# Layer 3's feed-forward: the gate product on VectorE out of its PSUM bank, and its steps in a new order

## What is computed

```
g = silu(einsum('th,ehi->tei', xf, w_gate))
u = einsum('th,ehi->tei', xf, w_up)
experts_y = einsum('tei,eih->teh', g * u, w_down)
y = sum over the 2 picked experts of experts_y * weight
shared = silu(x @ sw_gate) * (x @ sw_up) @ sw_down
x = x + tanh(g_ffn[3]) * (y + shared)
```

## Time and profile before

| | |
|---|---|
| runs | 932.77, 924.78, 932.22 us; median 932.22 |
| the profiled execution | 930.15 us, of which the span of its instructions is 928.4 us |
| PE busy | 841.6 us (91% of the span) |
| DVE busy | 763.0 us (82%) |
| ACT busy | 555.4 us (60%) |
| POOL busy | 309.8 us (33%) |

### The profile page before, as it was taken

How to read it: one execution, slowest core, us unless ns; L and a number is a source line. 1 busy time by engine, 2 the same in 40 slices (tenths; PEclk the granted TensorE clock), 3 DMA queues, 4 the chain that set the end, 5 groups by cost and what they waited for, 6 DMA issues and landing times.

```text
span 928.4 us, 16914 instructions
## 1 busy us (share of the span) xinstructions
PE 841.6 (91%) x5288; PEld 651.5 (70%) x5288; DVE 763.0 (82%) x1907; ACT 555.4 (60%) x1077; POOL 309.8 (33%) x507
## 2 busy tenths in 40 slices
PE   5998887899999999999999999999979989978796
PEld 3776756666666665688878788778767779867574
DVE  6899899869999998699889899788887755465886
ACT  3777565547777775675666565577755534423474
POOL 2644226313444433232222122433421253321143
PEclk9999999759999997999999999999998999997998
DMA  5000000000000000010000000020001000000001
GB/s 155 9 2 1 4 26 1 25 1 26 26 25 26 22 23 1 9 42 0 1 1 1 1 1 1 0 76 2 1 2 43 1 1 1 1 1 1 1 12 34
DMA packets 26005, 14.12 MB, mean 15 GB/s; under 512 B 11047, under 2 KB 25406, under 8 KB 25918
## 3 DMA queue, kind: packets, MB, share of 16 engines
q1 hardware_dynamic: 25758, 13.04, 5.1%
q10 hardware_dynamic: 160, 0.00, 0.0%
HBM read 11.99 MB, written 1.05 MB: 14 GB/s over the span
## 4 chain that ended last, share of the span: by engine, by line
PE 47%; DVE 8%; issue 3%; ACT 3%; POOL 0%; DVEq 0%; ACTq 0%; POOLq 0%
PE bank L1844 4%; PE bank L1846 3%; PE bank L1845 3%; PE bank L798 2%; PE bank L1319 2%; PE bank L1900 2%; PE bank L1901 2%; PE bank L1899 2%; PE bank L1274 2%; PE bank L1284 2%; PE bank L1297 1%; PE bank L1255 1%; PE bank L731 1%; PE bank L709 1%; PE bank L758 1%
## 5 line engine op out<-in xcount | busy, mean ns | idle before, releaser
L893 ACT ACTIVATE L_pt<-bank 128x512 f32<-128x512 f32 x224 | 127.2, 598 | 46.4 <-PE bank L767 32.5
L515 POOL TENSOR_TENSOR L_kc<-L_kc_all,const 128x256 fp32r<-128x256 f32 x96 | 59.7, 625 | 141.7 <-PE bank L767 81.9
L1026 DVE TENSOR_REDUCE L_ms<-bank 128x2 f32<-128x512 f32 x128 | 84.0, 685 | 11.8 <-PE bank L716 11.4
L1801 POOL TENSOR_TENSOR L1f_xg_lo<-L1f_xg_raw,L1f_xg_hi 128x512 fp32r<-128x512 f32 x32 | 42.0, 1313 | 145.3 <-ACT L1f_xg_hi L1949 141.3
L880 ACT ACTIVATE L_part<-bank,L_bias_ca,const 128x256 fp32r<-128x256 f32 x128 | 68.9, 563 | 33.8 <-PE bank L687 32.4
L2065 DVE TENSOR_TENSOR L1f_h_lo<-L1f_h,L1f_h_hi 128x512 fp32r<-128x512 f32 x88 | 75.2, 859 | 6.2 <-ACT L1f_h_hi L1954 5.9
L1943 ACT ACTIVATE L1f_a<-bank 128x512 f32<-128x512 f32 x88 | 52.4, 599 | 43.3 <-PE bank L1846 42.9
L1024 DVE TENSOR_REDUCE L_mc<-bank 128x8 f32<-128x512 f32 (+1 forms) x96 | 65.1, 678 | 8.7 <-PE bank L709 4.4
L1954 ACT CAST L1f_h_hi<-L1f_h 128x512 fp32r<-128x512 f32 x88 | 54.3, 618 | 18.8 <-DVE L1f_h L2060 18.8
L716 PE MATMUL bank<-L_k,L_q 32*128 32x256 f32 x256 | 55.9, 342 | 5.1 <-DVE L_ms L1026 4.9
L887 ACT ACTIVATE L_hm<-bank,const 128x256 fp32r<-128x256 f32 x96 | 45.6, 475 | 21.5 <-PE bank L731 20.6
(11 more groups left out here) (427 smaller groups left out, 2601.1 us busy)
## 6 DMA issues: line engine op xcount, KB each, us to landing
L_raw<-in_L_ffn_w_dram SPq DMA_DIRECT2D x8, 176.0 KB, 2.3
L_raw<-in_L_ffn_v_dram SPq DMA_DIRECT2D x8, 176.0 KB, 2.5
L_raw<-in_L_ffn_w_dram SPq DMA_DIRECT2D x6, 192.0 KB, 2.9
x<-in_x_dram SPq DMA_DIRECT2D x4, 256.0 KB, 4.3
mask<-in_mask_Bx1xSxS_ff_dram SPq DMA_DIRECT2D x2, 512.0 KB, 5.6
out_dram<-x SPq DMA_DIRECT2D x4, 256.0 KB, 2.3
const<-in_const_dram SPq DMA_DIRECT2D x1, 964.0 KB, 6.0
ctx_rows<-in_ctx_dram SPq DMA_DIRECT2D x1, 256.0 KB, 3.1
```

Of the source, the lines that this page charges most:

```text
L515: pool.tensor_tensor(kc[:, g], kc_all[:, g, bass.ds(b, 1)].bitcast(F32).to_broadcast([P, GH, S2]), pr.c("head4").unsqueeze(2).to_broadcast ...
L893: act.activation(pt[:, g // 2, (g % 2) * NS + (HEADS_1[i] if own_keys else i)], b_st[(g * NS + i) % 2][:], ACT.Exp, scale=scale).then_inc( ...
L1026: dve.tensor_reduce(ms[:, :, i - 1], bank.rearrange("p (t s) -> p t s", s=S), AX_X, ALU.max).then_inc(sem["sc_taken"], 1)
```

## The change

ACT's `gate` step and POOL's `mul` step go, and with them the tile `gb` and the semaphore `gate_copied`. DVE's `mul` step, which did nothing in layer 3, now multiplies `h` by the gates straight out of their bank. PE's `gate` matmul waits for the product of the gated chunk two before it, where it waited for the copy out of that bank.

```diff
 gpsimd:
-        def mul(n):
-            ...
-            pool.wait_ge(sem["gate_copied"], past["gate_copied"] + g + 1)
-            pool.tensor_tensor(h[:, n % RH], h[:, n % RH], gb[:, g % 2], ALU.mult).then_inc(sem["h_done"], 1)
 tensor, gate(n):
-                need(pe, sem["gate_copied"], g - 1, past["gate_copied"])
+                need(pe, sem["h_done"], GATED[g - 2] + 1 if g >= 2 else 0, past["h_done"])
             pe.matmul(b_gate[g % 2][:], sel[:, c * P:(c + 1) * P], gts[:, i], start=True, stop=True).then_inc(sem["gate_done"], 1)
 scalar:
-        def gate(n):
-            ...
-                act.copy(gb[:, g % 2], b_gate[g % 2][:]).then_inc(sem["gate_copied"], 1)
 vector:
         def mul(n):
             if layer == 3:
+                dve.wait_ge(sem["half_done"], past["half_done"] + n + 1)
+                if n not in GATED:
+                    dve.wait_ge(sem["h_done"], past["h_done"] + n)
+                    dve.sem_inc(sem["h_done"], 1)
+                    return
+                g = gated_before(n)
+                dve.wait_ge(sem["gate_done"], past["gate_done"] + g + 1)
+                dve.tensor_tensor(h[:, n % RH], h[:, n % RH], b_gate[g % 2][:], ALU.mult).then_inc(sem["h_done"], 1)
                 return
 PLACES, "tensor":
-        (('att3', 'divide', 7, 1), *of("ffn3", ('turn', 2), ('logits', 2)), *of("att3", ('y', 7))),
+        (('att3', 'pv', 7, 1), *of("ffn3", ('logits', 2)), *of("att3", ('y', 7))),
 ...
```

More of the change, by code:

```diff
@@ L2116, in ffn_wide @@
         3: (("lo", 12, 34, "xt_hi xt_lo xt_raw sel yt"), ("arena", 86, 108, "h xn mv ve rstd router extra total total2 total3"), ("hi", 25, 34, "a"),
[L2117 removed]
+            ("arena", 32, 48, "gx pe p1 cand top8 want left picked gs gtop gwant gleft"), ("arena", 0, 32, "gts h_hi h_lo hg"))}[layer])
     mv = sb("mv", [P, NT, 2])
@@ L2393, in y_copy @@
             act.copy(yt[:], b_y[:]).then_inc(sem["yt_ready"], 1)
-        return {"turn": turn, "route": route, "gates": gates, "up": up, "gate": gate, "split": split, "y_copy": y_copy}
+        return {"turn": turn, "route": route, "gates": gates, "up": up, "split": split, "y_copy": y_copy}
     def vector(dve):
@@ L2841 @@
[L2841 to L2854, removed]
+        (('att3', 'divide', 3, 1), *of("att3", ('pv', 3, 1))),
+        (('att3', 'weights', 4, 1), *of("att3", ('proj', 5, 1))),
@@ new lines @@
+        (('att3', 'divide', 4, 0), *of("att3", ('divide', 4, 1), ('turn', 6), ('pv', 4, 0))),
+        (('att3', 'weights', 5, 0), *of("att3", ('context_values', 6))),
+        (('att3', 'divide', 5, 0), *of("att3", ('divide', 5, 1), ('pv', 5, 0), ('turn', 7))),
+        (('att3', 'pv', 5, 1), *of("att3", ('context_values', 7), ('proj', 7, 0))),
+        (('att3', 'y', 5), *of("att3", ('divide', 6, 0))),
+        (('att3', 'maxima', 7), *of("att3", ('divide', 6, 1), ('pv', 6, 0))),
+        (('ffn3', 'logits', 0), *of("att3", ('sums', 7), ('pv', 7, 0))),
@@ new lines @@
+        (('att3', 'divide', 7, 0), *of("att3", ('divide', 7, 1)), *of("ffn3", ('turn', 2), ('logits', 1))),
+        (('att3', 'pv', 7, 1), *of("ffn3", ('logits', 2)), *of("att3", ('y', 7))),
+        (('ffn3', 'up', 1), *of("ffn3", ('up', 2), ('up', 3))),
+        (('ffn3', 'turn', 3), *of("ffn3", ('up', 4))),
+        (('ffn3', 'gates', 0), *of("ffn3", ('gate', 0))),
+        (('ffn3', 'up', 5), *of("ffn3", ('gate', 1))),
+        (('ffn3', 'gate', 3), *of("ffn3", ('up', 7), ('up', 8))),
+        (('ffn3', 'down', 0), *of("ffn3", ('up', 9), ('gates', 2), ('gate', 5))),
@@ new lines @@
+        (('ffn3', 'down', 2), *of("ffn3", ('up', 10))),
+        (('ffn3', 'gate', 6), *of("ffn3", ('gate', 7), ('up', 11))),
+        (('ffn3', 'down', 4), *of("ffn3", ('up', 12))),
+        (('ffn3', 'down', 5), *of("ffn3", ('up', 13), ('gate', 10), ('gate', 11), ('down', 6), ('down', 7), ('up', 14), ('up', 15))),
+        (('ffn3', 'y_turn', 0), *of("ffn3", ('gate', 12), ('gate', 13))),
+        (('ffn3', 'up', 17), *of("ffn3", ('gates', 3))),
+        (('ffn3', 'down', 8), *of("ffn3", ('down', 9))),
@@ L2950 @@
         (('att3', 'maxima', 3), *of("att3", ('turn', 4), ('p_moments', 3))),
+        (('att3', 'scores', 4, 0), *of("att3", ('parts', 3))),
         (('att3', 'maxima', 4), *of("att3", ('turn', 5))),
[L2952 to L2955, removed]
+        (('att3', 'divide', 3, 0), *of("att3", ('divide', 3, 1)), *of("ffn3", ('moments', 0))),
@@ new lines @@
+        (('att3', 'y', 3), *of("att3", ('turn', 6))),
+        (('att3', 'maxima', 5), *of("att3", ('scale', 7)), *of("ffn3", ('prepare',))),
+        (('att3', 'y', 4), *of("ffn3", ('scale', 0)), *of("att3", ('turn', 7))),
+        (('att3', 'scores', 7, 0), *of("att3", ('parts', 6))),
+        (('att3', 'scores', 7, 1), *of("ffn3", ('moments', 1))),
+        (('att3', 'divide', 6, 1), *of("ffn3", ('moments', 2))),
+        (('att3', 'parts', 7), *of("ffn3", ('turn', 0), ('turn', 1))),
+        (('att3', 'divide', 7, 0), *of("att3", ('divide', 7, 1)), *of("ffn3", ('turn', 2))),
@@ L2972 @@
+        (('ffn3', 'gates', 3), *of("ffn3", ('up', 17), ('mul', 15), ('mul', 16))),
+        (('ffn3', 'split', 15), *of("ffn3", ('up', 19))),
+        (('ffn3', 'mul', 17), *of("ffn3", ('mul', 18), ('y_turn', 1), ('mul', 19))),
+        (('ffn3', 'split', 19), *of("ffn3", ('y_turn', 2))),
     ),
@@ L3071 @@
-        (('ffn3', 'up', 17), *of("ffn3", ('gate', 12))),
-        (('ffn3', 'split', 11), *of("ffn3", ('gate', 13))),
-        (('ffn3', 'y_copy', 1), *of("ffn3", ('gate', 15), ('gate', 16))),
-        (('ffn3', 'gate', 14), *of("ffn3", ('up', 18))),
-        (('ffn3', 'split', 14), *of("ffn3", ('gate', 17), ('gate', 18), ('up', 19))),
+        (('att3', 'turn', 6), *of("att3", ('maxima', 5), ('weights', 5, 0))),
+        (('att3', 'divide', 4, 1), *of("att3", ('context_values', 6))),
+        (('att3', 'maxima', 6), *of("att3", ('turn', 7))),
```

177 lines of the change are left out of this document (83 added, 94 removed).

## The result

The changed kernel takes 919.73 us in the median of four runs (914.95 to 920.66), the kernel before 932.5 (924.78 to 932.78): a ratio of 0.9873, 95% interval 0.9833 to 0.9913, so 1.3% faster. That lies inside the range 908 to 922.5, on the side that was forecast. The profiled execution took 914.95 us (span 913.2), against the 915.1 that the sum gave for it.

What follows compares the result with a forecast made beforehand. Attention up to y 5 was taken as PE-bound, A as held up by PE's wait for L3f_xn, C as VectorE's work plus waiting. 930.15 - 12.5 (A) - 2.55 (C) = 915.1 us, range 908 to 922.5.

Steps and rivals of the forecast that it cites:

- A: Stretch from y of batch 5 to the end of layer 3's last y: 31.46 us becomes 19.0, 12.5 less.
- the hole: In A, PE's 7.86 us wait for L3f_xn, until 837.92 us, expected to go.
- three waits: Late waits allowed in A: m_split 0.2 us, divide 7 and logits 2 0.3 each, 0.8 together.
- `prepare` at no cost: In attention batches, VectorE's five-instruction block fits into a 5.66 us wait; without that cover 2.9 us.
- B: Stretch behind A, 16.85 us, where VectorE routes tokens: nothing gained, at best 1.4 us.
- the tail: From the last h_lo to the last addition, 4.90 us: same chain, nothing gained.
- VectorE's work in C: In C, 37.25 us plus 9.6 for 16 products minus 8.6 for faster h_lo gives 38.25.
- C: Feed-forward proper, 44.30 us: VectorE's 38.25 of work plus 3.5 idle gives 41.75, 2.55 less.
- (1): Rival: hole in A goes but little else, A 23.6 and C 45.3 us, total 923.3; chance 0.09.
- (2): Rival in C: VectorE and PE in lockstep at each gate, 9.6 us longer, total 924.7; chance 0.07.
- (3): Rival in the attention: VectorE stands waiting for POOL's rstd and PE loses time, ending above 941.5 us; chance 0.02.
- (4): Rival: B or the tail absorbs A's gain because VectorE sets A's end, no change to measure; chance 0.02.

Runs made afterwards that it cites:

- e1: Kernel before with the new order only up to the end of layer 3's attention, old gate copy and product kept; median 916.0 us, ratio 0.9851.
- e6: Changed kernel with moments 0, rstd 0 and scale 0 back behind the division of batch 6, prepare still early; median 923.07 us, ratio 0.9924.
- e11: Kernel before with the new order only up to the end of the attention, measured a second time; median 916.9 us, ratio 0.9849.
- e4: Changed kernel without the 16 products by the gates, VectorE still waiting and signalling; median 916.0 us, ratio 0.9848.
- e7: Changed kernel with up 5 moved ahead of gate 0 on TensorE; median 914.31 us, ratio 0.9822.
- e10: The changed kernel itself, unaltered, measured again; median 917.5 us, ratio 0.9861.
- e3: Kernel before in its old order, only the gate product moved from GpSimd to VectorE, some one or two steps earlier; median 939.4 us, ratio 1.0083.
- e2: Changed kernel with the old order up to y 7, keeping the VectorE product and new order of the 20 chunks; median 929.6 us, ratio 1.0003.
- e9: Changed kernel with several up matmuls and VectorE's up products earlier, scale 3 and group 3's transposes not delayed; median 914.9 us, ratio 0.9824.
- e5: Changed kernel plus 16 GpSimd products nobody reads, each behind a gated chunk's up product; median 922.39 us, ratio 0.9920.

## Why the prediction came out right, step by step

- **A (19.0 predicted, 18.81 measured).** Right in mechanism and size, and shown: e1 has it without the rest of the change, e6 gives half of the hole back with the chain alone. The 18.2 us of work at full clock were 18.8, and none of the three waits for which 0.8 was allowed came: PE is busy the whole stretch. That these two misses cancel is luck.
- **`prepare` at no cost.** Right. The selector's copy took 427 ns at 805.32 us, as in layer 0 and not the 1742 of the earlier trace rows; GpSimd's fill had run from 783.45 to 785.26, 20 us earlier. The prediction took a wait of 5.66 us in every batch for the room; that is the longest of six, the others in the kernel before are 3.60 to 5.27, which still covers the 2.9 of the block.
- **B (nothing) and the tail (nothing).** B right in its length, 16.96. But its contents changed: PE has 46 matmuls there for 57, because `up` 5 and 6 now stand behind gate 0, which waits for the end of B. I compared VectorE's list in B and not PE's. The tail was 1.5 us shorter, which I had not seen. The same code as before takes 3.90 there in e1 and e11, at a clock of 1.00; so 1.0 of the 1.5 goes with the lower clock at the end of the profile before, which left PE 17 matmuls in the tail for e1's 14. The other 0.5 goes with the new order, which leaves 10.
- **VectorE's work in C (38.25 predicted, 38.61 measured).** Right term by term: the product costs as much as the `h_lo` without GpSimd beside it (683 and 687 ns), no dearer for its input in a bank, so the estimate of 1.0 us more by the access times of the Trainium skill (Perfetto Trace Analysis, "Optimizing Scalar/DVE Operations") did not come; `h_lo` 13.2 us for the 12.4 that were taken.
- **C (41.75 predicted, 43.90 measured).** This is the step that failed: "C becomes 38.25 + 3.5" takes VectorE as what sets the end of C. With `up` 5 and 6 in it and half the clock for its first 3.1 us, PE has 42.62 us to do there, and VectorE's idle time became 5.3 us instead of 3.5: 1.8 of it is waiting for `gate`'s bank, 1.5 for silu's output, which waits for PE's `up`. e4 shows that VectorE's work matters by 1 us at most there, e7 and e10 that PE's does. Of the 2.55 us expected, 0.34 came, and none against the old code's C in e1 and e11 (43.4), which ran at a clock of 1.00.
- **The sum.** 915.1 against 914.95 in the profile is closer than its parts, and that is luck: 2.2 us too much in C stand against 1.5 in the tail and 0.8 of a `y` 5 that came earlier by itself. By the medians the gain was 12.8 us for the 15 forecast, since the profiled run was the lowest of its four.
- **The rivals.** (1) did not happen: the clock stood at 1.00 through A. (2) did not happen in this kernel, but e3 is that rival: its C is 53.93 us, where the price of 9.6 on top of the forecast 41.75 gives 51.35. Its condition was the order of the chunks, which is the part of the change that keeps it away. (3): VectorE waited 0.41 us once for `rstd`, nothing behind it was late. (4) did not happen: A's gain reached the end in full (e1).
- **What the change consists of.** The prediction gave 12.5 of 15 us to the order in the attention and 2.55 to the product. The runs give 12.65 to the order in A, and to the product with its own order nothing that the medians show: alone, at the places that e3 gave it, the product costs 8 to 10 us, which the chunks' order gives back (e2).

## What to carry to other kernels

Price a stretch by each engine's list in it, after the change: a step that leaves one stretch for the next takes its time along, and here two `up` chunks moved past a wait made PE the bound that VectorE was taken for. When one diff holds a new way of computing and a new order, take them apart, each alone and in the old order, before the gain is put down to either. A wait in an in-order engine is free for work that stands behind it and can stand ahead of it: moving six matmuls in front of it was worth 2 us here, about half of it by the clock.

## What the runs showed of the hardware

- The granted clock often fell behind PE's idle times, and that comes on top of the idle time: in the changed kernel 3.46 us of idle time were followed, half a microsecond later, by 3.4 us of matmuls at half the rate, and 1.82 us by 3.1 us at a clock of 0.50; 0.42 us in e7 by none. But the length of the idle time alone does not tell. The same 1.82 us were followed by 5.7 us at 0.50 in e10; 0.89 us by 3.4 us at 0.53 in the kernel before and by no fall in e1; and in e9 the clock fell for 3.0 us though PE had waited 0.77 and 0.16 us in the 3.7 us ahead of that.
- Most of the scatter of the whole time comes from ahead of `y` 5 (its start varies by 9.5 us, the rest of the changed kernel by 1.5), and part of it from the granted clock there. From 200 to 400 us the changed kernel and e9 have this (columns as above), and e9's `y` 5 starts 9.5 us later:

```profile
200.00:400.00 200.00, 188.13 (x1568) 127.52 (x1567) 179.26 (x442) 142.50 (x288) 77.91 (x158) 0.95 0.09 23
```

```profile
200.00:400.00 200.00, 188.18 (x1527) 125.05 (x1528) 171.50 (x429) 137.26 (x279) 73.53 (x153) 0.89 0.06 17
```

- VectorE's 128x512 operation with two inputs in SBUF went from 0.68 to as much as 1.79 us beside a GpSimd product (e5), one with an input in PSUM did not go above 0.69. It is not only operations with two inputs: in e5 a TENSOR_SCALAR of 128x4 (L2489) took 1.07 us beside such a product, for 0.17 in the changed kernel.
